# A sparse feed-forward layer whose first matmul writes features on partitions

## Chip, cores, metric

The kernel runs on one core of a Trainium2 chip. The metric is the device time of one execution in microseconds; the median of several runs counts. The kernel is written by hand: each engine (TensorE for matmuls, called PE in the profile; VectorE, DVE; ScalarE, ACT; GpSimd, POOL; SyncE, SP) has its own list of instructions, and semaphores tie them together.

## The reference

A small transformer of eight sub-layers, each adding to x (16 sequences, 112 positions, 256 features) what it makes of layernorm(x): cross-attention (0), feed-forward (1), attention (2), feed-forward (3), attention (4), feed-forward (5), attention (6), feed-forward (7). Sub-layers 1, 5 and 7 are mixtures of 8 experts, and they are what the change touches:

```
sub-layer 1: expert = argmax of the router,    F = 1024, func = gelu
sub-layer 5: the best two experts of 8,        F = 512,  func = silu
sub-layer 7: expert = argmax of the router,    F = 256,  func = gelu
out = weight * (func(x @ W1[e] + b1[e]) @ W2[e] + b2[e])      W1: 256 x F, W2: F x 256
```

The reference computes all experts for all rows; the kernel computes for each row only the experts it is sent to.

## The kernel before

`route_phase` makes the layernorm, the router's choice, and stores each row's 256 features in DRAM as two float16 parts (HI, and LO, the rest). `experts_phase` sorts the rows by expert into tiles of 128 rows that belong to one expert each: NT is 21 tiles in sub-layer 1, 35 in sub-layer 5 and 21 in sub-layer 7. Which expert a tile has is known only at run time: PE loads its number into a register (`value_load`, L2449) and every access to the expert's weights is addressed through a register (`bass.ds(e, 1)`).

For each tile j the engines do this:

- POOL gathers 128 rows from DRAM (`gather`, L2335), XR + 3 tiles ahead.
- PE turns the gathered rows (`turn_x`, L2363: four transposes of 128x128 in float16), and DVE copies them out of PSUM to `x16` (`take_x`, L2535): features on partitions, in HI and LO parts.
- `hidden` (L2372 to L2388): for each block of BW = min(F, 512) hidden features, one matmul that adds the bias (`add_bias`, L2368 or L2370, with 2 or 16 partitions), and six matmuls (x LO by w HI, x HI by w LO, x HI by w HI, each in two halves of the 256 features). The stationary operand is `x16` (128x128), the moving one the weights w1h, BW columns. The result in PSUM has rows on partitions.
- ACT applies the function (`apply`, L2469) into `hs`, which lies in the space of XT.
- The result has to be turned before the second layer, since its features must be on partitions. For F = 1024 `turn_h` (L2407) turns the float32 result in 8 transposes, ACT takes the HI part from PSUM (`high_h`, L2490), DVE the LO part (`low_h`, L2551). For F = 512 and 256 (`early`) ACT and DVE first make the two float16 parts (`high_parts` L2476, `low_parts` L2539), PE turns both (`turn_parts`, L2396, 2F/128 transposes), and ACT and DVE copy them out (`take_high` L2482, `take_low` L2545) to `h16`.
- `output` (L2411 to L2427): F/128 matmuls of 512 columns (L2420), a bias matmul (L2368 or L2370) and F/128 matmuls of 256 columns (L2424), with `h16` stationary and w2h moving.
- ACT copies half of the result (`half_y`, L2496), DVE adds the other (`add_y`, L2558), POOL scatters the rows to DRAM (L2346).

The order of each engine's work is written out by hand in its loop over j. On PE it is: load the expert of tile j, `turn_x(j + 1)`, `hidden(j)`, turn the result of tile j - 1, `output(j - 2)`. In between ACT and DVE also turn the experts' weights, which SP loads as float32, into the float16 parts: `make_high` (L2064) on ACT and `make_low` (L2070) on DVE, four pieces per expert for F = 1024 and two otherwise.

Of the kernel before, what the change touches and what calls it, by code (L numbers as in the profile page):

```python
# [16 lines left out]
DC = D // 128  # L17
# [2228 lines left out]
def experts_phase(nc, tag, X, XT, ident, r, w, xnd, ytd, func, xn=None, out=None):  # L2246
# [5 lines left out]
    HR, YR = 3, 3  # L2252
# [3 lines left out]
    with ExitStack() as st:  # L2256
# [17 lines left out]
        h16 = m.sb("h16", [128, 2, 2, F], F16)  # L2274
        y2 = m.sb("y2", [128, 2, D])
        if F == 1024:
            xs = XT[:, 1, 1024:1024 + XR * D].bitcast(F16).rearrange("p (r d) -> p r d", d=2 * D)
            y = XT[:, 0, 1024:1024 + YR * D].rearrange("p (r d) -> p r d", d=D)
        else:
            xs, y = m.sb("xs", [128, XR, 2 * D], F16), m.sb("y", [128, YR, D])  # L2280
            hk = m.sb("hk", [128, 2, 2, F], F16)
# [10 lines left out]
        t_bank = [(m.bank16 if early else m.bank)(f"t{i}") for i in range(2)]  # L2292
# [8 lines left out]
        turned, x_ready, h_done, h_made, t_done, h_hi, h_low, o_done, y_half, y_done, x_done, added = (  # L2301
            m.sem(n) for n in ("turned", "x_ready", "h_done", "h_made", "t_done", "h_hi", "h_low", "o_done", "y_half",
                               "y_done", "x_done", "added"))
        hk_hi, hk_low, ready16, stored = m.sem("hk_hi"), m.sem("hk_low"), m.sem("ready16"), m.sem("stored")
# [5 lines left out]
        with nc.Block() as block:  # L2310
# [42 lines left out]
            def _(pe):  # L2353
# [17 lines left out]

                def hidden(j):  # L2372
                    e = experts[j]
                    pe.wait_ge(x_ready, j + 1)
                    pe.wait_ge(w.split, upto(min(j, E - 1) - 1) + w.first)
                    for blk in range(NB):
                        n = j * NB + blk
                        bank = h_bank[n % HR]
                        cols = slice(blk * BW, (blk + 1) * BW)
                        if n >= HR:  # L2380
                            pe.wait_ge(h_made, n - HR + 1)
                        add_bias(bank[:, 0:BW], e, cols, start=True, stop=False)
                        for i, (x, z) in enumerate(PARTS):
                            for c in range(DC):
                                mm = pe.matmul(bank[:, 0:BW], x16[:, j % 2, x, c, :],  # L2385
                                               w.w1h[:, z, c, bass.ds(e, 1), cols].rearrange("p o f -> p (o f)"),
                                               start=False, stop=(i, c) == (2, DC - 1))
                        mm.then_inc(h_done, 1)  # L2388

                def turn_parts(j):  # L2390
                    pe.wait_ge(hk_low, j + 1)
                    for z in (HI, LO):
                        if j >= 1:
                            pe.wait_ge((h_hi, h_low)[z], j)
                        for f in range(FC):
                            mm = pe.transpose(t_bank[z][:, f * 128:(f + 1) * 128], hk[:, j % 2, z, f * 128:(f + 1) * 128],  # L2396
                                              ident16[:, :])
                        mm.then_inc(t_done, 1)

                def turn_h(j):  # L2400
                    pe.wait_ge(h_made, (j + 1) * NB)
                    for blk in range(NB):
                        if j * NB + blk >= 2:
                            pe.wait_ge(h_low, j * NB + blk - 1)
                        for f in range(BW // 128):
                            at = blk * BW + f * 128
                            mm = pe.transpose(t_bank[(j * NB + blk) % 2][:, f * 128:(f + 1) * 128], hs[:, j % 2, at:at + 128],  # L2407
                                              ident[:, :])
                        mm.then_inc(t_done, 1)

                def output(j):  # L2411
                    e = experts[j]
                    bank = o_bank[j % 2]
                    pe.wait_ge(w.split, upto(min(j, E - 1)))
                    pe.wait_ge(h_hi, (j + 1) * NB)
                    pe.wait_ge(h_low, (j + 1) * NB)
                    if j >= 2:
                        pe.wait_ge(y_done, j - 1)
                    for f in range(FC):
                        pe.matmul(bank[:, :], h16[:, j % 2, HI, f * 128:(f + 1) * 128],  # L2420
                                  w.w2h[:, bass.ds(e, 1), f, :, :].rearrange("p o z d -> p (o z d)"), start=f == 0, stop=False)
                    add_bias(bank[:, 0:D], e, slice(F, F + D), start=False, stop=False)
                    for f in range(FC):
                        mm = pe.matmul(bank[:, 0:D], h16[:, j % 2, LO, f * 128:(f + 1) * 128],  # L2424
                                       w.w2h[:, bass.ds(e, 1), f, HI, :].rearrange("p o d -> p (o d)"), start=False,
                                       stop=f == FC - 1)
                    mm.then_inc(o_done, 1)  # L2427
# [19 lines left out]
                for j in range(NT + 2):  # L2447
                    if j < NT:
                        experts[j] = pe.value_load(tile_expert[0:1, j:j + 1], min_val=0, max_val=E - 1)  # L2449
                    if j + 1 < NT:  # L2450
                        turn_x(j + 1)
                    if j < NT:
                        hidden(j)
                    if 1 <= j < NT + 1:
                        (turn_parts if early else turn_h)(j - 1)
                    if j >= 2:
                        output(j - 2)

            @block.scalar
            def _(act):  # L2460
                def apply(j):
                    if j >= 2 and early:
                        act.wait_ge(hk_low, j - 1)
                    elif j >= 2:
                        act.wait_ge(t_done, (j - 1) * NB)
# [6 lines left out]
                def high_parts(j):  # L2472
                    act.wait_ge(h_made, j + 1)
                    if j >= 2:
                        act.wait_ge(t_done, 2 * (j - 1))
                    act.copy(hk[:, j % 2, HI, :], hs[:, j % 2, :]).then_inc(hk_hi, 1)  # L2476

                def take_high(j):
                    act.wait_ge(t_done, 2 * j + 1)
                    if j >= 2:  # L2480
                        act.wait_ge(o_done, j - 1)
                    act.copy(h16[:, j % 2, HI, :], t_bank[HI][:, 0:F]).then_inc(h_hi, 1)  # L2482

                def high_h(j):
                    if j >= 2:
                        act.wait_ge(o_done, j - 1)
                    for blk in range(NB):
                        n = j * NB + blk
                        act.wait_ge(t_done, n + 1)
                        act.copy(h16[:, j % 2, HI, blk * BW:(blk + 1) * BW], t_bank[n % 2][:, 0:BW]).then_inc(h_hi, 1)  # L2490
# [11 lines left out]
                for j in range(NT + 2):  # L2502
# [3 lines left out]
                    if j < NT:  # L2506
                        apply(j)
                        if early:
                            high_parts(j)
                    if 1 <= j < NT + 1:  # L2510
                        (take_high if early else high_h)(j - 1)
                    if j >= 2:
                        half_y(j - 2)
# [5 lines left out]
            def _(dve):  # L2519
# [17 lines left out]
                def low_parts(j):  # L2537
                    dve.wait_ge(hk_hi, j + 1)
                    dve.tensor_tensor(hk[:, j % 2, LO, :], hs[:, j % 2, :], hk[:, j % 2, HI, :], ALU.subtract).then_inc(hk_low, 1)  # L2539

                def take_low(j):
                    dve.wait_ge(t_done, 2 * j + 2)
                    if j >= 2:
                        dve.wait_ge(o_done, j - 1)
                    dve.tensor_copy(h16[:, j % 2, LO, :], t_bank[LO][:, 0:F]).then_inc(h_low, 1)  # L2545

                def low_h(j):
                    for blk in range(NB):
                        n = j * NB + blk
                        dve.wait_ge(h_hi, n + 1)  # L2550
                        dve.tensor_tensor(h16[:, j % 2, LO, blk * BW:(blk + 1) * BW], t_bank[n % 2][:, 0:BW],  # L2551
                                          h16[:, j % 2, HI, blk * BW:(blk + 1) * BW], ALU.subtract).then_inc(h_low, 1)
# [91 lines left out]
                for j in range(NT + 2):  # L2644
# [5 lines left out]
                    if early and j < NT:  # L2650
                        low_parts(j)
                    if 1 <= j < NT + 1:
                        (take_low if early else low_h)(j - 1)
                    if j >= 2:
                        add_y(j - 2)
# [139 lines left out]
```

## Time and profile before

| | |
|---|---|
| median of 3 runs | 2612.92 us (2605.26 to 2613.96) |
| the profiled execution's own time | 2597.31 us |
| its span | 2595.4 us |
| granted TensorE clock over the span | 0.917 of full speed |
| PE, DVE, ACT, POOL busy | 85%, 61%, 53%, 37% |
| experts' tiles of sub-layer 1 on PE | 331 to 490 us |
| of sub-layer 5 | 1999 to 2145 us |
| of sub-layer 7 | 2518 to 2575 us |

In the profile PE is the matmul side of TensorE and PEld its weight loads, which overlap with matmuls. A matmul's duration holds its way through the array, so durations of neighbours overlap; what counts is the distance from one start to the next.
### The profile page before, as it was taken

How to read it: one execution, taken by the hardware profiler on the slowest of the kernel's cores; microseconds unless marked ns; L12 is line 12 of the kernel's file. 1: busy time of each engine (PE TensorE's matmuls, PEld its weight loads, DVE VectorE, ACT ScalarE, POOL GpSimd, SP SyncE). 2: the span in 40 equal slices, each digit the busy share in tenths (PEclk: the TensorE clock that was granted, in tenths of full speed). 3: DMA queues.
4: the chain of work that ended last, by engine and by line, in shares of the span. 5: the costliest groups of instructions: out<-in, count | busy, mean ns of one | idle time of the engine just before them, and what ended most of it. 6: DMA issues, size and time to landing. Idle time of an engine off the chain costs nothing. (4 is left out here: it accounts for less than half of the span.)

```text
span 2595.4 us, 62474 instructions
## 1 busy us (share of the span) xinstructions
PE 2197.0 (85%) x23896; PEld 1460.3 (56%) x23896; DVE 1573.8 (61%) x3664; ACT 1381.3 (53%) x2919; POOL 955.7 (37%) x1066
## 2 busy tenths in 40 slices
PE   4888499689999999958689999999974993899846
PEld 2556245367777777745546666666652551466524
DVE  3667572476665656636767777777765644555465
ACT  2666463265555555524366666666653652566634
POOL 3543132154454444403423333333313742433135
PEclk7999699899999999968889999999986996899958
DMA  5663271310000000010200000000023224432034
GB/s 118 118 111 78 87 237 35 106 36 14 14 8 14 14 14 2 2 33 1 81 14 15 14 15 9 15 14 9 2 71 95 78 60 113 98 79 68 21 110 127
DMA packets 118580, 139.57 MB, mean 54 GB/s; under 512 B 15072, under 2 KB 107184, under 8 KB 118288
## 3 DMA queue, kind: packets, MB, share of 16 engines
q1 hardware_dynamic: 110900, 115.39, 17.3%
q0 software_dynamic: 7392, 20.19, 2.5%
q8 instruction: 199, 3.26, 0.6%
q14 instruction: 89, 0.73, 0.1%
HBM read 93.25 MB, written 17.47 MB: 43 GB/s over the span
## 5 line engine op out<-in xcount | busy, mean ns | idle before, releaser
L915 DVE TENSOR_REDUCE a_mx<-a_pair 112x2 f32<-112x750 f32 x256 | 237.9, 936 | 196.0 <-PE a_pair L984 196.0
L1223 POOL TENSOR_TENSOR a_kp<-a_kp 125x512 f16<-125x512 f32 x192 | 217.6, 1159 | 259.1 <-ACT a_kp L1314 259.1
L316 POOL TENSOR_SCALAR a_P<-a_P,a_inv 112x375 f32<-112x375 f32 x256 | 148.9, 595 | 378.1 <-DVE a_inv L447 377.0
L853 ACT ACTIVATE a_PT<-a_pair 125x672 f32<-125x672 f32 x256 | 186.3, 731 | 69.9 <-PE a_pair L996 65.2
L354 ACT ACTIVATE a_P<-a_masked,a_least 112x375 f32<-112x375 f32 x256 | 153.4, 600 | 83.5 <-DVE a_least L442 81.6
L1357 DVE SCALAR_TENSOR_TENSOR a_k<-a_p,a_k 128x375 f16<-128x375 f32 x128 | 69.3, 547 | 138.9 <-ACT a_k L1270 138.8
L1314 ACT CAST a_kp<-a_kp 125x512 f16<-125x512 f32 x192 | 110.4, 617 | 76.4 <-DVE a_kp L1376 76.4
L535 PE MATMUL a_p<-a_kc,a_wk 128*128 128x375 f16 x768 | 147.0, 327 | 4.1 <-POOL a_kc L310 4.1
L1456 PE MATMUL a_p<-a_kc,a_wk 128*128 128x375 f16 x768 | 142.2, 327 | 5.4 <-POOL a_kc L1215 5.4
L442 DVE CUSTOM_DVE_ANT_0 a_masked<-a_s,a_mask_add 112x375 f32<-112x375 f32 x256 | 129.9, 545 | 27.1 <-PE a_s L572 26.1
L549 PE MATMUL a_p<-a_wv,a_kc 128*125 128x512 f16 x576 | 141.9, 383 | 5.2 <-DVE a_v L481 3.6
L1456 PE MATMUL a_p<-a_wv,a_kc 128*125 128x512 f16 x576 | 141.0, 385 | 0.0
L2385 PE MATMUL f_hb<-w_w1h,f_x 128*128 x588 | 136.7, 371 | 0.0
L2469 ACT ACTIVATE all_XT<-f_hb 128x512 f32<-128x512 f32 (+1 forms) x98 | 53.3, 550 | 152.6 <-PE f_hb L2385 151.4
L1376 DVE TENSOR_SCALAR a_kp<-a_p 125x512 f32<-125x512 f32 x192 | 122.8, 681 | 8.2 <-PE a_p L1487 8.2
L472 DVE SCALAR_TENSOR_TENSOR a_k<-a_p,a_k 128x375 f16<-128x375 f32 x128 | 70.3, 549 | 82.7 <-ACT a_k L365 82.7
L582 PE MATMUL a_t<-all_ident,a_P 112*125 112x112 f32 x768 | 116.5, 288 | 3.4 <-POOL a_P L316 3.4
L452 DVE TENSOR_TENSOR a_PT<-a_t,a_PT 125x336 f16<-125x336 f32 x256 | 116.8, 498 | 1.4 <-ACT a_PT L390 1.4
L582 PEld LDWEIGHTS a_t<-all_ident,a_P 112*125 112x125 f32 x768 | 93.8, 188 | 38.8 <-issue 34.6
L1015 PE MATMUL a_y<-a_PT,a_values 125*32 125x112 f32 x3072 | 102.4, 267 | 5.4 <-ACT a_PT L853 5.3
L549 PEld LDWEIGHTS a_p<-a_wv,a_kc 128*125 128x125 f16 x576 | 77.8, 137 | 49.7 <-DVE a_k L472 6.8
L996 PE MATMUL a_pair<-a_q,a_k 50*125 50x112 f16 (+1 forms) x1536 | 89.2, 223 | 19.5 <-DMA a_q<-a_mT 10.9
(420 smaller groups left out, 5271.1 us busy)
## 6 DMA issues: line engine op xcount, KB each, us to landing
a_kc<-in_ctxT SPq DMA_DIRECT2D x64, 375.0 KB, 3.4
a_k<-a_k_parts SPq DMA_DIRECT2D x192, 93.8 KB
w_stage<-in_L_ffn_W SPq DMA_DIRECT2D x32, 512.0 KB, 5.5
w_stage<-in_L_ffn_ew SPq DMA_DIRECT2D x16, 512.0 KB, 5.9
w_stage<-expert_rows SPq DMA_DIRECT2D x16, 448.0 KB, 7.6
a_v_in_sb<-in_ctx SPq DMA_DIRECT2D x16, 375.0 KB
a_q<-a_q_parts SPq DMA_DIRECT2D x48, 112.0 KB, 3.5
w_stage<-in_L_ffn_W SPq DMA_DIRECT2D x16, 256.0 KB, 4.5
```

The lines of the kernel that those rows point to most:

```text
L316: pool.tensor_scalar(P[:, p % 4, r, :], P[:, p % 4, r, :], inv[:, p % 4, r:r + 1], 1.0, ALU.mult, ALU.mult).then_inc(P_done, 1)
L354: act.activation(P[:, p % 4, r, :], masked[:, p % 2, r, :], ACT.Exp, bias=least[:, p % 4, r:r + 1], scale=-1.0, accum_out=total[:, p % 4, ...
L442: dve.tensor_tensor_reduce(masked[:, p % 2, r, :], s_bank[0:S, r, 0:SK], mask_add[:, b % 2, :], 1.0, 3e38, ALU.add, ALU.min, least[:, p % ...
L535: mm = pe.matmul(out[:, 0:SK], wk16[:, z, j, c * 128:(c + 1) * 128], kc16[:, b % 2, x, j, :], start=i == j == 0, stop=(i, j) == (2, DC - 1))
L549: mm = pe.matmul(out[0:KP, 0:512], kc16[:, b % 2, x, j, jk * KP:(jk + 1) * KP], wv16[:, z, j, w * 512:(w + 1) * 512], start=i == j == 0, s ...
L582: mm = pe.transpose(t_bank[0:KP, r, j * S:(j + 1) * S], P[:, p % 4, r, j * KP:(j + 1) * KP], ident[0:S, 0:S])
L853: act.activation(PT[:, p % 4, :, :], pair_bank[slot["turned", p]][0:KP, :, 0:KT * S], ACT.Exp).then_inc(exp_done, 1)
L915: dve.tensor_reduce(mx[:, b % 2, 2 * pair:2 * pair + 2], pair_bank[slot["score", p]][0:S, :, 0:SK], AX.X, ALU.max).then_inc(max_done, 1)
L1223: pool.tensor_tensor(kp16[:, LO, j, hf, r, :, :].rearrange("p c m -> p (c m)"), kp[:, n % 4, :], kp16[:, HI, j, hf, r, :, :].rearrange("p ...
L1376: dve.tensor_scalar(kp[:, n % 4, :], p_bank[bank][0:KP, 0:512], 0.0, EPS * WS, ALU.max, ALU.add).then_inc(f_evac, 1)
L1456: mm = pe.matmul(out, lhs(x, z, j), rhs(x, z, j), start=i == j == 0, stop=(i, j) == (2, DC - 1))
L2385: mm = pe.matmul(bank[:, 0:BW], x16[:, j % 2, x, c, :], w.w1h[:, z, c, bass.ds(e, 1), cols].rearrange("p o f -> p (o f)"), start=False, st ...
```

## The change

The first layer is computed the other way round. In `hidden` the weights w1h are now the stationary operand, 128 hidden features at a time, and the 128 rows of `x16` move; so a block of 512 hidden features, seven matmuls of 512 columns before, becomes four groups of seven matmuls of 128 columns. Each group begins with its own bias matmul (`turn_bias`), whose stationary operand is the bias row and whose moving operand is a row of ones (or `r.pick`). Each group writes 128 columns of the same PSUM bank. The result has features on partitions, so `turn_h` and `turn_parts` are gone, with `hk`, the banks `t_bank`, and the copies `high_parts`, `low_parts`, `take_high` and `take_low`; `high_h` and `low_h` now make the parts from `hs` for all F. For F = 1024 the outputs run one tile behind the first layer rather than two (LATE); for F = 512 and 256 still two, with three buffers in `h16`. HR, the number of banks for the first layer, is 4 rather than 3.

```diff
@@ experts_phase
     early = F < 1024
-    HR, YR = 3, 3
+    HR, YR = 4, 3
+    LATE = 2 if early else 1
+    HB = LATE + 1
...
-        h16 = m.sb("h16", [128, 2, 2, F], F16)
+        h16 = m.sb("h16", [128, HB, 2, F], F16)
...
-            hk = m.sb("hk", [128, 2, 2, F], F16)
...
-        t_bank = [(m.bank16 if early else m.bank)(f"t{i}") for i in range(2)]
...
+                def turn_bias(out, e, cols):
+                    if w.flat:
+                        pe.matmul(out, w.rows[:, bass.ds(e, 1), cols].rearrange("z o f -> z (o f)"), ones16[:, :], start=True, stop=False)
+                    else:
+                        pe.matmul(out, w.rows[:, cols], r.pick[:, bass.ds(e, 1), :].rearrange("p o t -> p (o t)"), start=True,
+                                  stop=False)
+
                 def hidden(j):
...
-                        cols = slice(blk * BW, (blk + 1) * BW)
                         if n >= HR:
                             pe.wait_ge(h_made, n - HR + 1)
-                        add_bias(bank[:, 0:BW], e, cols, start=True, stop=False)
-                        for i, (x, z) in enumerate(PARTS):
-                            for c in range(DC):
-                                mm = pe.matmul(bank[:, 0:BW], x16[:, j % 2, x, c, :],
-                                               w.w1h[:, z, c, bass.ds(e, 1), cols].rearrange("p o f -> p (o f)"),
-                                               start=False, stop=(i, c) == (2, DC - 1))
-                        mm.then_inc(h_done, 1)
-
-                def turn_parts(j):
...
-                def turn_h(j):
...
                         for f in range(BW // 128):
                             at = blk * BW + f * 128
...
+                            out = bank[:, f * 128:(f + 1) * 128]
+                            turn_bias(out, e, slice(at, at + 128))
+                            for c in range(DC):
+                                for x, z in ((HI, HI), (LO, HI), (HI, LO)):
+                                    mm = pe.matmul(out, w.w1h[:, z, c, bass.ds(e, 1), at:at + 128].rearrange("p o f -> p (o f)"),
+                                                   x16[:, j % 2, x, c, :], start=False, stop=(c, z) == (DC - 1, LO))
+                        mm.then_inc(h_done, 1)
...
-                for j in range(NT + 2):
+                for j in range(NT + LATE):
...
                         hidden(j)
-                    if 1 <= j < NT + 1:
-                        (turn_parts if early else turn_h)(j - 1)
-                    if j >= 2:
-                        output(j - 2)
+                    if j >= LATE:
+                        output(j - LATE)
...
                 def apply(j):
-                    if j >= 2 and early:
-                        act.wait_ge(hk_low, j - 1)
-                    elif j >= 2:
-                        act.wait_ge(t_done, (j - 1) * NB)
+                    if j >= 2:
+                        act.wait_ge(h_low, (j - 1) * NB)
...
-                def high_parts(j):
...
-                def take_high(j):
...
                 def high_h(j):
-                    if j >= 2:
-                        act.wait_ge(o_done, j - 1)
+                    if j >= HB:
+                        act.wait_ge(o_done, j - HB + 1)
                     for blk in range(NB):
...
+                        act.wait_ge(h_made, j * NB + blk + 1)
+                        act.copy(h16[:, j % HB, HI, blk * BW:(blk + 1) * BW],
+                                 hs[:, j % 2, blk * BW:(blk + 1) * BW]).then_inc(h_hi, 1)
...
-                def low_parts(j):
...
-                def take_low(j):
...
                 def low_h(j):
                     for blk in range(NB):
...
+                        cols = slice(blk * BW, (blk + 1) * BW)
+                        dve.wait_ge(h_hi, j * NB + blk + 1)
+                        dve.tensor_tensor(h16[:, j % HB, LO, cols], hs[:, j % 2, cols], h16[:, j % HB, HI, cols],
+                                          ALU.subtract).then_inc(h_low, 1)
```

## Rows read from the trace of the kernel before

**Rows 1.** Windows, one each in sub-layers 1, 5, 7: PE, PEld, DVE, ACT, POOL busy, granted clock

```profile
355.00:475.00 120.00, 120.00 (x694) 63.97 (x693) 49.84 (x80) 54.22 (x97) 33.27 (x31) 1.00 0.26 84
2062.00:2130.00 68.00, 68.00 (x477) 36.42 (x476) 30.27 (x68) 35.17 (x68) 34.47 (x36) 1.00 0.22 65
2550.23:2562.15 11.92, 11.92 (x102) 7.62 (x100) 6.97 (x21) 7.17 (x21) 9.18 (x10) 1.00 0.39 106
```

**Rows 2.** Timeline of PE in one tile of sub-layer 1 (start, us, what)

```profile
460.68 0.39 PE L2363 MATMUL f_xt<-f_ident,all_XT 128*128 128x128 f16 x4
461.00 0.39 PE L2370 MATMUL f_hb<-w_rows,r_pick 16*128 16x512 f16 x1
461.32 1.47 PE L2385 MATMUL f_hb<-w_w1h,f_x 128*128 x6
...
464.34 1.04 PE L2407 MATMUL f_t<-all_ident,all_XT 128*128 128x128 f32 x8
465.21 1.89 PE L2420 MATMUL f_o<-w_w2h,f_h 128*128 x8
...
468.13 0.39 PE L2363 MATMUL f_xt<-f_ident,all_XT 128*128 128x128 f16 x4
```

**Rows 3.** Timeline of PE in one tile of sub-layer 5

```profile
2057.36 0.39 PE L2363 MATMUL f_xt<-f_ident,f_xs 128*128 128x128 f16 x4
2057.68 0.39 PE L2368 MATMUL f_hb<-w_rows,f_ones 2*128 x1
...
2059.31 0.61 PE L2396 MATMUL f_t<-f_ident,f_hk 128*128 128x128 f16 x8
2059.75 1.03 PE L2420 MATMUL f_o<-w_w2h,f_h 128*128 x4
...
2061.37 0.33 PE L2363 MATMUL f_xt<-f_ident,f_xs 128*128 128x128 f16 x3
```

**Rows 4.** Timeline of PE in one tile of sub-layer 7

```profile
2550.55 0.28 PE L2368 MATMUL f_hb<-w_rows,f_ones 2*128 x1
...
2551.43 0.39 PE L2396 MATMUL f_t<-f_ident,f_hk 128*128 128x128 f16 x4
2551.65 0.59 PE L2420 MATMUL f_o<-w_w2h,f_h 128*128 x2
...
2552.62 0.39 PE L2363 MATMUL f_xt<-f_ident,f_xs 128*128 128x128 f16 x4
```

**Rows 5.** Instructions of single lines: duration min/median/max, first and last start

```profile
L2420 PEldq FUSED_REGOPS  x8: 46/46/46, 462.9 to 463.9; - x8
...
L2385 PEld LDWEIGHTS f_hb<-w_w1h,f_x x588: 95/98/147, 331.6 to 2570.1; 128*128 128x128 f16 x196
...
L2385 PEldq FUSED_REGOPS  x392: 46/46/46, 330.8 to 2569.6; - x196
...
L2449 PEldq TENSOR_LOAD <-f_tile_expert x17: 300/302/310, 2063.1 to 2127.2; - x17
...
L2359 PEldq EVENT_SEMAPHORE  x17: 51/51/51, 2063.8 to 2127.9; - x17
```

**Rows 6.** Bias matmuls L2368 in sub-layers 5 and 7: first and last start

```profile
L2368 PE MATMUL f_hb<-w_rows,f_ones x35: 384/385/602, 1999.5 to 2137.6; 2*128 x35
...
L2368 PE MATMUL f_hb<-w_rows,f_ones x21: 277/278/391, 2518.3 to 2569.4; 2*128 x21
```

**Rows 7.** Timeline of PE in sub-layer 2: a run of short matmuls

```profile
704.04 1.25 PE L1517 MATMUL a_kvs_sum<-a_v,a_kp 125*128 125x65 f16 x36
705.22 0.75 PE L1497 MATMUL a_p<-a_q,a_pp 64*128 64x224 f16 x12
```

**Rows 8.** Groups by line of ACT and DVE, 355 to 475 us

```profile
L2064 ACT ACTIVATE w_w2h<-w_stage 128x1024 f16<-128x1024 f32 x7 | 7.4, 1061 | 5.1 <-DMA w_stage<-in_L_ffn_W 5.1
...
L2070 DVE SCALAR_TENSOR_TENSOR w_w2h<-w_stage,w_w2h 128x1024 f16<-128x1024 f32 x8 | 9.6, 1220 | 2.6 <-ACT w_w2h L2064 2.6
```

**Rows 9.** Timeline of POOL in sub-layer 7

```profile
2544.84 0.99 POOL L2346 DMA_INDIRECT expert_rows<-f_y,f_dest  x1 [0.31 <-issue]
```

More of the change, by code:

```diff
@@ L2300, in experts_phase @@
         got_in = [m.sem(f"got_in{i}") for i in range(G)]
-        turned, x_ready, h_done, h_made, t_done, h_hi, h_low, o_done, y_half, y_done, x_done, added = (
-            m.sem(n) for n in ("turned", "x_ready", "h_done", "h_made", "t_done", "h_hi", "h_low", "o_done", "y_half",
+        turned, x_ready, h_done, h_made, h_hi, h_low, o_done, y_half, y_done, x_done, added = (
+            m.sem(n) for n in ("turned", "x_ready", "h_done", "h_made", "h_hi", "h_low", "o_done", "y_half",
                                "y_done", "x_done", "added"))
-        hk_hi, hk_low, ready16, stored = m.sem("hk_hi"), m.sem("hk_low"), m.sem("ready16"), m.sem("stored")
+        ready16, stored = m.sem("ready16"), m.sem("stored")
         def upto(e):
@@ L2388, in hidden @@
-                        mm.then_inc(h_done, 1)
-                def turn_parts(j):
[L2391 to L2398, printed above, removed]
@@ L2400, in turn_h @@
-                def turn_h(j):
[L2401 to L2404, printed above, removed]
                         for f in range(BW // 128):
                             at = blk * BW + f * 128
-                            mm = pe.transpose(t_bank[(j * NB + blk) % 2][:, f * 128:(f + 1) * 128], hs[:, j % 2, at:at + 128],
-                                              ident[:, :])
-                        mm.then_inc(t_done, 1)
+                            out = bank[:, f * 128:(f + 1) * 128]
@@ L2419, in output @@
                     for f in range(FC):
-                        pe.matmul(bank[:, :], h16[:, j % 2, HI, f * 128:(f + 1) * 128],
+                        pe.matmul(bank[:, :], h16[:, j % HB, HI, f * 128:(f + 1) * 128],
                                   w.w2h[:, bass.ds(e, 1), f, :, :].rearrange("p o z d -> p (o z d)"), start=f == 0, stop=False)
@@ L2423, in output @@
                     for f in range(FC):
-                        mm = pe.matmul(bank[:, 0:D], h16[:, j % 2, LO, f * 128:(f + 1) * 128],
+                        mm = pe.matmul(bank[:, 0:D], h16[:, j % HB, LO, f * 128:(f + 1) * 128],
                                        w.w2h[:, bass.ds(e, 1), f, HI, :].rearrange("p o d -> p (o d)"), start=False,
@@ L2470, in apply @@
                                        scale=1.0 / WS).then_inc(h_made, 1)
-                def high_parts(j):
-                    act.wait_ge(h_made, j + 1)
-                    if j >= 2:
-                        act.wait_ge(t_done, 2 * (j - 1))
-                    act.copy(hk[:, j % 2, HI, :], hs[:, j % 2, :]).then_inc(hk_hi, 1)
-                def take_high(j):
-                    act.wait_ge(t_done, 2 * j + 1)
-                    if j >= 2:
-                        act.wait_ge(o_done, j - 1)
-                    act.copy(h16[:, j % 2, HI, :], t_bank[HI][:, 0:F]).then_inc(h_hi, 1)
                 def high_h(j):
-                    if j >= 2:
-                        act.wait_ge(o_done, j - 1)
+                    if j >= HB:
+                        act.wait_ge(o_done, j - HB + 1)
                     for blk in range(NB):
-                        n = j * NB + blk
-                        act.wait_ge(t_done, n + 1)
-                        act.copy(h16[:, j % 2, HI, blk * BW:(blk + 1) * BW], t_bank[n % 2][:, 0:BW]).then_inc(h_hi, 1)
+                        act.wait_ge(h_made, j * NB + blk + 1)
+                        act.copy(h16[:, j % HB, HI, blk * BW:(blk + 1) * BW],
+                                 hs[:, j % 2, blk * BW:(blk + 1) * BW]).then_inc(h_hi, 1)
                 def half_y(j):
@@ L2501, in _ @@
                 act.activation(warm[:, :], ident[:, 0:1], func)
-                for j in range(NT + 2):
+                for j in range(NT + LATE):
                     if not early:
@@ L2507, in _ @@
                         apply(j)
[L2508 to L2513, printed above, removed]
+                        high_h(j)
+                    if j >= LATE:
+                        half_y(j - LATE)
                     if early:
@@ L2535, in take_x @@
                     dve.tensor_copy(x16[:, j % 2, :, :, :].rearrange("p z c t -> p (z c t)"), xt_bank[:, 0:2 * D]).then_inc(x_ready, 1)
-                def low_parts(j):
-                    dve.wait_ge(hk_hi, j + 1)
-                    dve.tensor_tensor(hk[:, j % 2, LO, :], hs[:, j % 2, :], hk[:, j % 2, HI, :], ALU.subtract).then_inc(hk_low, 1)
-                def take_low(j):
[L2542 to L2545, printed above, removed]
                 def low_h(j):
                     for blk in range(NB):
[L2549 to L2552, printed above, removed]
+                        cols = slice(blk * BW, (blk + 1) * BW)
+                        dve.wait_ge(h_hi, j * NB + blk + 1)
+                        dve.tensor_tensor(h16[:, j % HB, LO, cols], hs[:, j % 2, cols], h16[:, j % HB, HI, cols],
+                                          ALU.subtract).then_inc(h_low, 1)
                 def add_y(j):
@@ L2643, in _ @@
                 take_x(0)
-                for j in range(NT + 2):
+                for j in range(NT + LATE):
                     if j + 1 < NT:
@@ L2649, in _ @@
                             w.make_low(dve, n)
[L2650 to L2655, printed above, removed]
+                    if j < NT:
+                        low_h(j)
+                    if j >= LATE:
+                        add_y(j - LATE)
                     if early:
```

## The prediction

> **What bounds the kernel now.** I read the table of the page first, then windows over the three expert stages, then the timeline of PE in one steady tile of each, and last the single lines of PE's sequencer. The windows [rows 1] show PE busy without a gap in all three stages at a granted clock of 1.00 (the 2.4 GHz level), while DVE, ACT and POOL are busy for 28 to 77% of them. So a tile costs what PE takes for it: 468.13 - 460.68 = 7.45 us in sub-layer 1 [rows 2], 2061.37 - 2057.36 = 4.01 us in sub-layer 5 [rows 3], and 2.39 us in sub-layer 7: 2552.62 - 2550.55 = 2.07 from the bias matmul to the next `turn_x` [rows 4], and 0.32 for `turn_x`, as in the other two (461.00 - 460.68, 2057.68 - 2057.36). Only there is POOL slower: one scatter of 0.99 us with 0.31 us ahead of it, and a gather of the same size, make 2.6 us per tile [rows 9], but it catches up once the gathers are through, so PE sets the end there too.
>
> Two prices come out of these rows. Eight transposes of 128 columns take 2059.75 - 2059.31 = 0.44 us [rows 3], so a 128-column matmul costs 0.056 us start to start. In sub-layer 1 the first block's bias matmul is 0.32 us ahead of the next one, and `hidden` with its 14 matmuls lasts 464.34 - 461.00 = 3.34 us [rows 2]. With p for a 512-column matmul and s for a change of shape between the 16-partition bias and the 128-partition matmuls, p + s = 0.32 and 14p + 3s = 3.34, which gives p = 0.216 and s = 0.10. The four transposes of `turn_x`, 4 x 0.056 = 0.22, again last 0.32 up to the bias matmul: s is paid on entering and on leaving a bias matmul, with 2 partitions in sub-layer 5 and 7 as well [rows 3, 4].
>
> **The array's part of the change.** The columns that stream stay the same: 7 x 512 before, 28 x 128 after. What changes is the number of bias matmuls. A new group costs 0.056 + s, five times 0.056, and 0.056 + s to the next bias: 0.59 us. `hidden` then takes 8 x 0.59 - 0.10 = 4.61 us in sub-layer 1, 4 x 0.59 - 0.10 = 2.26 in 5, and 2 x 0.59 - 0.10 = 1.08 in 7.
> - Sub-layer 1: +1.27 against 3.34; the transposes go, 465.21 - 464.34 = 0.87 [rows 2]. Net +0.40, tile 7.85 us.
> - Sub-layer 5: +0.63 against 2059.31 - 2057.68 = 1.63; 0.44 goes [rows 3]. Net +0.19, tile 4.20 us.
> - Sub-layer 7: +0.20 against 0.88; 2551.65 - 2551.43 = 0.22 goes [rows 4]. Net 0, tile 2.37 us.
>
> So the transposes saved are paid back by six further changes of shape per 512 hidden features.
>
> **The sequencer's part.** An address that depends on the expert is computed by a FUSED_REGOPS. `hidden` has 392 of them in 98 blocks, four per block, one for each pair of z and c, and the repeated w HI addresses share theirs; `output` has eight per tile of sub-layer 1, one for each f [rows 5]. So each new constant offset costs one, and the change makes the offset depend on f as well: 4 per group, 16 per 512 features instead of 4, plus the bias's one per group where `w.rows` is addressed by expert (sub-layers 5 and 7; in 1 `r.pick` has one address per tile). Eight in a row start within 463.9 - 462.9 us, 7 distances [rows 5]: 0.13 us each with the pair of load and matmul behind it. Loading the expert's number costs 2063.8 - 2063.1 = 0.7 us up to the next wait [rows 5], and I give the four separate waits that remain (one of `turn_parts` goes) 0.13 each. Sequencer per tile:
> - Sub-layer 1: before 8 + 8 + 1 addresses, after 32 + 8 + 1: 41 x 0.13 + 0.7 + 0.5 = 6.5 us, under the array's 7.85.
> - Sub-layer 5: before 5 + 5, after 20 + 5: 25 x 0.13 + 1.2 = 4.45 us, over the array's 4.20. I take 4.40, since the distances are rounded to 0.1 us.
> - Sub-layer 7: before 5 + 3, after 10 + 3: 13 x 0.13 + 1.2 = 2.9 us, over 2.37. I take 2.80. POOL's 2.6 is now hidden.
>
> An address for a weight load is in no row (so far only moving operands have one). Below it could be free if the load needs none, above it is as dear as a moving one's; I take the upper end, the nearest row, and keep the lower one for a rival.
>
> **Waits and other engines.** ACT and DVE lose one PSUM copy each per tile in 5 and 7; in 1 the same copies read `hs`. None is late before: per tile of sub-layer 1 ACT has four pieces of 1.06 us and DVE four of 1.22 [rows 8], 4.2 and 4.9 us, with some 2.8 and 2.1 us besides, under 7.85. With outputs one tile behind, PE's `output(j - 1)` comes after `hidden(j)`, 4.6 us after `hidden(j - 1)` and `output(j - 2)`, so ACT and DVE have time to make the parts. On DVE `low_h(j)` now stands ahead of `add_y`, and behind it the next `take_x`, which PE needs only an iteration later; I cost it at nothing, covered by `output`'s 2.92 us in sub-layer 1 and 1.6 in 5 [rows 2, 3]. Without that cover it would be the length of `low_h`, an estimated 0.6 us per 512 columns, half of the 1.22 us [rows 8]. POOL and SP issue the same DMAs. The fourth first-layer bank only loosens a wait.
>
> **The sum.** Sub-layer 1: 21 x 0.40 = +8.4. In 5 the 35 tiles began on average (2137.6 - 1999.5) / 34 = 4.06 us apart [rows 6], so 34 x 0.34 = +11.6. In 7 it was (2569.4 - 2518.3) / 20 = 2.56 [rows 6], so 20 x 0.24 = +4.8. The first matmuls of a stage run at the lower clock (602 ns at most against 385 [rows 6]), with more of them in each group: +1. In all +26 us. The profiled execution took 2597.3 us, 15.6 under the median; on the median this makes 2639 us. A measurement of this kernel can tell about 0.3%, 8 us, from no change.
>
> The page "TensorE: Matmul & The Clock Gate" of the Trainium skill, section "Back-to-back issue gap", speaks against short matmuls: it gives some 81 ns for each of a stream of loads and 128-column matmuls. The trace has 56 ns in runs of eight [rows 3]. By 81 ns a group would cost 0.77 us and the sum would come to about +73 us; this belongs beside the first rival.
>
> **Rivals.**
> 1. *Weight loads set the pace* (9%). Each 128-column matmul needs its own load of 98 ns [rows 5]; if loads with an address in a register did not overlap with each other, a group would take 7 x 0.098 + 0.10 = 0.79 us. Tiles: 0.32 + 8 x 0.79 - 0.1 + 2.92 = 9.46, 0.31 + 3.06 + 1.62 = 4.99, 0.32 + 1.48 + 0.97 = 2.77 us: 21 x 2.0 + 34 x 0.93 + 20 x 0.21 = +78 us, 2691. Against it stand 36 matmuls of 65 columns with their loads in 1.18 us, 33 ns each [rows 7].
> 2. *The clock falls* (5%). The array streams for 7 x 0.053 of 0.59 us, less densely than now. At 1.2 GHz the 128-column matmul costs 0.107 and a group 0.95, 0.36 us more: tiles of 10.7, 5.6 and 3.1 us, 21 x 3.3 + 34 x 1.6 + 20 x 0.5 = +134 us, 2747. Against it: 33 ns matmuls ran at full pace in sub-layer 2 [rows 7].
> 3. *Faster* (13%): the change of shape is hidden when short matmuls stand around the bias, and the new addresses cost the sequencer nothing to speak of. A group is then 7 x 0.056 = 0.39 us. Sub-layer 1: 0.32 + 3.14 + 2.92 = 6.38, -1.07 x 21 = -22; sub-layer 5: 0.31 + 1.57 + 1.62 = 3.50, -0.56 x 34 = -19; sub-layer 7 is held by POOL, -1: -42 us, 2571. It decides once a group costs less than (3.34 + 0.87 + 0.10) / 8 = 0.54 us in sub-layer 1 and fewer than (4.06 - 1.2) / 0.13 = 22 addresses are left per tile in 5. For it speaks only that the rows have no group of this form.
> 4. *About even* (8%): changes of shape free, addresses as forecast. Sub-layer 1 is at the sequencer's 6.5, -20; 5 and 7 as forecast, +16: -4 us, 2609.
>
> If only the addresses were free, it would be +8.4 + 0.14 x 34 + 0 = +13 us; that lies in the forecast's own range, +12 to +45 us (upper end: sequencer and array hinder each other by 0.3 us per tile).
>
> **How the numbers follow.** The forecast has 65%. The range starts at 2608, between the even case and the forecast, which leaves out the faster rival, and reaches to 2685, short of the loads' full price: some 19% outside. Faster by over 0.3%: 0.13. Slower: forecast, loads and clock, 79%, less 4% of the forecast that ends within 8 us: 0.75. Same: 0.12.
>
> **What would show it.** On PE's timeline a tile of sub-layer 1 should take 7.85 us, of 5 4.4 and of 7 2.8; groups of L2370/L2368 and six matmuls should come every 0.59 us in sub-layer 1 and 0.65 in 5. FUSED_REGOPS of `hidden` should number 16 x 77 + 8 x 21 = 1400, with PE idle "issue" in 5 and 7. The page of lines should have no f_t. Groups of 0.39 us would make me wrong towards faster, loads 98 ns apart or a clock under 0.9 in these stages towards slower.

## The result, and the profile after

The changed kernel takes 2636.11 us in the median of four runs (2633.73 to 2642.45) against 2609.09 us before: 1.0111 times as estimated from all runs, 95% interval [1.0094, 1.0129] (the two medians alone divide to 1.0104). The change makes the kernel 1% slower. The prediction was 2639 against 2613, 1.0100 times. The profiled execution of the change took 2635.8 us with a span of 2633.7.

One tile of sub-layer 1 on PE's timeline, where [rows 2] stood before:

```profile
412.92 0.39 PE L2363 MATMUL f_xt<-f_ident,all_XT 128*128 128x128 f16 x4
413.24 0.22 PE L2376 MATMUL f_hb<-r_pick,w_rows 16*128 x1
413.39 0.51 PE L2394 MATMUL f_hb<-f_x,w_w1h 128*128 128x128 f16 x6
413.83 0.23 PE L2376 MATMUL f_hb<-r_pick,w_rows 16*128 x1
...
417.93 1.89 PE L2407 MATMUL f_o<-w_w2h,f_h 128*128 x8
...
420.84 0.39 PE L2363 MATMUL f_xt<-f_ident,all_XT 128*128 128x128 f16 x4
```

A group of seven comes every 413.83 - 413.24 = 0.59 us, 0.15 to 0.16 us of it from the bias matmul to the next and as much back again, where 0.056 us would do without a change of shape. `hidden` takes 417.93 - 413.24 = 4.69 us (forecast 4.61), `output` still 2.91, the tile 7.92 us (forecast 7.85, before 7.45). The transposes are gone (0.87 us), but `hidden` is 1.35 us longer: the six further changes of shape per 512 hidden features cost more than the transposes did.

The weight loads show where a change of shape costs its time. These are loads of the change, then of the padded kernel e3 below, in which no matmul changes the shape:

```profile
413.23 0.09 PEld L2376 LDWEIGHTS f_hb<-r_pick,w_rows 16*128 16x128 f16 x1
413.39 0.34 PEld L2394 LDWEIGHTS f_hb<-f_x,w_w1h 128*128 x6
```

```profile
405.67 0.10 PEld L2382 LDWEIGHTS f_hb<-r_pick,w_rows 128*128 128x128 f16 x1
405.73 0.38 PEld L2400 LDWEIGHTS f_hb<-f_x,w_w1h 128*128 x6
```

In e3 each load starts some 0.055 us ahead of its own matmul (405.73 and 405.78 on PE), right behind the start of the matmul before it. In the change the loads at 413.23 and 413.39 start at the same time as their matmuls: at a change of shape the load is not made ahead, and that holds for the bias matmul's load and for the one after it.

One tile of sub-layer 5, for [rows 3], and the lines of the first layer, for [rows 5]:

```profile
2077.53 0.39 PE L2363 MATMUL f_xt<-f_ident,f_xs 128*128 128x128 f16 x4
2077.85 0.23 PE L2374 MATMUL f_hb<-f_ones,w_rows 2*128 2x128 f16 x1
...
2080.24 1.03 PE L2407 MATMUL f_o<-w_w2h,f_h 128*128 x4
...
2081.86 0.39 PE L2363 MATMUL f_xt<-f_ident,f_xs 128*128 128x128 f16 x4
```

```profile
L2394 PEld LDWEIGHTS f_hb<-f_x,w_w1h x2100: 95/98/151, 330.0 to 2608.8; 128*128 x191
...
L2394 PEldq FUSED_REGOPS  x1400: 46/46/46, 329.5 to 2608.7; - x175
```

Addresses number 1400, as forecast, and this tile takes 4.33 us, others of the second half of the stage up to 4.62; the median of 34 distances is 4.45 (forecast 4.40, before 4.01). The loads keep their 98 ns with an address in a register. In the steady tiles of sub-layers 1 and 5 neighbours within a group are 0.056 us apart in the median, so neither short matmuls nor such loads are slow in themselves.

What was not forecast stands at the start of sub-layer 1. Windows of the kernel before, then of the changed one (start and end, length, PE, PEld, DVE, ACT, POOL busy, granted clock, DMA):

```profile
331.00:337.00 6.00, 6.00 (x17) 1.75 (x16) 5.59 (x8) 0.60 (x1) 0.95 (x1) 0.54 0.53 158
337.00:343.00 6.00, 6.00 (x37) 3.07 (x36) 4.36 (x5) 4.98 (x6) 0.96 (x1) 1.00 0.91 297
343.00:350.00 7.00, 7.00 (x42) 3.77 (x41) 6.74 (x8) 6.33 (x11) 0.00 (x0) 1.00 0.95 312
```

```profile
331.00:337.00 6.00, 6.00 (x45) 4.12 (x46) 3.81 (x4) 0.60 (x1) 0.04 (x1) 0.50 0.73 231
337.00:343.00 6.00, 6.00 (x47) 4.12 (x45) 4.18 (x8) 5.42 (x8) 0.96 (x1) 0.50 0.48 165
343.00:350.00 7.00, 7.00 (x44) 4.07 (x44) 4.00 (x5) 2.40 (x7) 0.00 (x0) 0.67 0.89 293
```

Both begin at the lower level, 1.2 GHz. Before, the clock is at 2.4 GHz (1.00) from 337 us on; with the change it stays at 0.50 until after 343, though PE counts as busy in both. At the lower level a group takes 0.97 us rather than 0.60.

### The profile page after: what moved, and what is told of

It is laid out like the page before. It is cut to its first block and busy times, and to the rows that moved or that the text cites. A ratio compares the mean times of both kernels' runs of the same rounds, so it can differ in the third digit from the quotient of the medians.

```text
span 2633.7 us, 65801 instructions
## 1 busy us (share of the span) xinstructions
PE 2230.4 (85%) x25128; PEld 1515.7 (58%) x25128; DVE 1558.2 (59%) x3608; ACT 1357.7 (52%) x2863; POOL 953.6 (36%) x1066
## 5 line engine op out<-in xcount | busy, mean ns | idle before, releaser
L2394 PE MATMUL f_hb<-f_x,w_w1h 128*128 128x128 f16 x2100 | 191.8, 231 | 0.6 <-issue 0.5
L2509 DVE TENSOR_TENSOR f_h<-all_XT,f_h 128x512 f16<-128x512 f32 (+1 forms) x98 | 60.3, 634 | 195.9 <-ACT f_h L2460 175.7
L2394 PEld LDWEIGHTS f_hb<-f_x,w_w1h 128*128 x2100 | 127.9, 102 | 27.6 <-issue 1.0
```

Of the source, the lines that this page charges most:

```text
L2394: mm = pe.matmul(out, w.w1h[:, z, c, bass.ds(e, 1), at:at + 128].rearrange("p o f -> p (o f)"), x16[:, j % 2, x, c, :], start=False, stop= ...
```

## The experiments

Seven kernels ran, in two groups, each on one chip; the kernel before took 2594.07 us beside the first four and 2607.06 beside the last three, so runs of different groups are compared by their ratios. This table has from each profile the median tile (distance from one `turn_x` to the next) and the length of each stage, from the start of the first `turn_x` to the end of the last `output`, in us, and the ratio of the times to the kernel before with its interval:

| | sub-layer 1 | sub-layer 5 | sub-layer 7 | ratio |
|---|---|---|---|---|
| before | 7.45, 163.6 | 4.01, 155.5 | 2.38, 59.9 | |
| change, first profile | 7.93, 178.8 | 4.45, 172.3 | 3.18, 74.8 | 1.0111 [1.0094, 1.0129] |
| e1 change again | 7.93, 179.1 | 4.45, 172.2 | 2.83, 68.9 | 1.0141 [1.0121, 1.0161] |
| e2 fixed expert | 7.93, 177.7 | 4.23, 165.5 | 2.39, 60.9 | 1.0095 [1.0075, 1.0114] |
| e3 change, padded | 6.71, 149.0 | 4.45, 168.1 | 2.79, 63.7 | 1.0017 [1.0003, 1.0030] |
| e4 before, padded | 6.83, 151.5 | 3.59, 143.0 | 2.33, 57.8 | 0.9902 [0.9874, 0.9931] |
| e5 e3 and one bias address | 6.71, 149.1 | 4.07, 158.4 | 3.24, 74.3 | 0.9946 [0.9929, 0.9962] |
| e6 e4, new form in 1 | 6.72, 149.2 | 3.59, 142.6 | 3.00, 69.7 | 0.9876 [0.9853, 0.9899] |
| e7 all one behind | 7.93, 178.4 | 4.47, 170.8 | 3.22, 74.4 | 1.0127 [1.0104, 1.0150] |

**e1, the change again.** No edit.

> The changed kernel once more, as a control. Theory (shape changes of 0.10 us around each bias matmul bound sub-layer 1, address computation bounds 5 and 7): tiles of 7.93, 4.43 and about 2.8 us; 2636 us. The first profile's sub-layer 7 had tiles of 2.7 to 4.7 us; if that comes from something that varies from run to run, these tiles differ here while those of 1 and 5 stay; if it belongs to the kernel, the same long tiles are at the same places.

2630.99 us. Sub-layers 1 and 5 repeat to 0.3 us. In 7 the long tiles of the first profile are not there: its second half runs at 2.73 to 2.87 us per tile. So the forecast 2.8 us is the kernel's, and the rest varies from run to run.

**e2, addresses constant.** It leaves out the choice of expert in the first layer, in 5 and 7 for the bias too.

```diff
-                        pe.matmul(out, w.rows[:, bass.ds(e, 1), cols].rearrange("z o f -> z (o f)"), ones16[:, :], start=True, stop=False)
+                        pe.matmul(out, w.rows[:, 0, cols], ones16[:, :], start=True, stop=False)
...
-                                    mm = pe.matmul(out, w.w1h[:, z, c, bass.ds(e, 1), at:at + 128].rearrange("p o f -> p (o f)"),
+                                    mm = pe.matmul(out, w.w1h[:, z, c, min(j, E - 1), at:at + 128],
...
```

> The first layer's weights (and in sub-layers 5 and 7 its bias) are those of expert min(j, 7) rather than of the tile's expert, so the first layer is that of another expert for most tiles and its addresses are constants. Theory: sub-layer 1 is bound by the array and stays at 7.9 us per tile; sub-layer 5 falls from 4.43 to the array's 4.2 us, sub-layer 7 from 2.8 to POOL's 2.6 us or a little under; about 2618 us. Rival (loads with an address in a register are slow in themselves): sub-layer 1 falls as well, by over 0.3 us per tile.

2618.82 us, 12 less than e1. Sub-layer 1 stays at 7.93, 5 falls to the array's 4.23 and 7 to 2.39. That is under POOL's 2.6, as it is in the kernel before (2.38): PE goes ahead of POOL while gathered tiles are in store. The addresses cost 0.22 us per tile in 5 and 0.4 in 7, nothing in 1.

**e3, no change of shape.** All operands of bias matmuls have 128 partitions, those beyond the bias filled with zeros.

```diff
-        self.pick = m.sb("pick", [2 * E, E, 128], F16)
+        self.pick = m.sb("pick", [128, E, 128], F16)
...
-        self.rows = m.sb("rows", [2, E, F + D] if self.flat else [2 * E, F + D], F16)
+        self.rows = m.sb("rows", [128, E, F + D] if self.flat else [128, F + D], F16)
...
+        pool.memset(self.rows[:], 0.0).then_inc(self.rows_blank, 1)
...
-        ident16, ones16, warm = m.sb("ident16", [128, 128], F16), m.sb("ones16", [2, 128], F16), m.sb("warm", [128, 1])
+        ident16, ones16, warm = m.sb("ident16", [128, 128], F16), m.sb("ones16", [128, 128], F16), m.sb("warm", [128, 1])
...
```

> The change with the operands of all bias matmuls filled up with zeros to 128 partitions, so that no matmul changes the shape of the array. Theory: groups of 0.39 us (7 x 0.056), the array would need 6.1 us in sub-layer 1, so that the sequencer's 6.5 us is the bound there; sub-layers 5 and 7, bound by the sequencer already, stay at 4.4 and 2.8. Together 21 x 1.4 = 30 us less than the change, 2606 us. Rival (short matmuls or their loads cost the time, not the shape): groups stay over 0.55 us and the time within 5 us of the change.

2597.94 us, 33 less than e1 (forecast 30). PE's timeline in sub-layer 1:

```profile
405.73 0.22 PE L2382 MATMUL f_hb<-r_pick,w_rows 128*128 x1
405.78 0.50 PE L2400 MATMUL f_hb<-f_x,w_w1h 128*128 128x128 f16 x6
406.12 0.22 PE L2382 MATMUL f_hb<-r_pick,w_rows 128*128 x1
```

The group is 0.39 us, as forecast to the hundredth. The tile is 6.71 rather than 6.5: the last groups of a tile come 0.5 us and more apart, as PE waits for addresses. Sub-layer 5 keeps 4.45, bound by the sequencer alone now. This row has eight addresses of one stretch of sub-layer 1:

```profile
L2400 PEldq FUSED_REGOPS  x8: 46/46/46, 400.6 to 401.5; - x8
```

By the trace's single starts (400.641 to 401.510) they are 0.124 us apart, although each lasts 46 ns, and the step is the same whether one pair of load and matmul stands between two of them or two. Some steps of a tile are longer, 0.15 to 0.28 us. In sub-layer 5 the 25 addresses make 3.1 of the 4.45 us; loading the expert's number takes 0.65 of the rest.

And the windows at the start of sub-layer 1, which here begins at 319.5 us:

```profile
319.00:326.00 7.00, 2.72 (x25) 2.49 (x26) 2.31 (x5) 1.06 (x1) 4.11 (x4) 0.50 0.61 208
326.00:332.00 6.00, 5.54 (x80) 4.97 (x78) 5.45 (x10) 3.81 (x6) 0.95 (x1) 0.94 0.82 262
```

The clock is up 7 us after the first `turn_x`, where the change took 23 and the kernel before 11. The matmuls are those of the change, in the same order; only the padding differs, and with it the pauses.

**e4, the same padding in the kernel before.** The edit of e3, nothing else.

> The kernel before with the same zeros in the bias operands and nothing else. Theory: six changes of shape of 0.10 us go per tile of sub-layer 1 (7.45 to 6.85 us), four in 5 (4.01 to 3.6), four in 7 (2.39 to 2.0, where POOL's 2.6 takes over): 13 + 14 + 1 us less than before, 2581 us. Rival (the 0.10 us comes from the bias matmul's other operands or its address, not from its few partitions): no change, 2609 us.

2566.80 us, 27 less than before (forecast 28). Tiles are 6.83, 3.59 and 2.33 us, the stages 12.1, 12.5 and 2.1 us shorter. In 7 PE gains 0.05 us per tile where the four changes of shape would give 0.4. It is not POOL's 2.6 that holds it, as the expectation had it, but the sequencer: in steady tiles its instructions follow one another without a pause, eight addresses of 0.124 us and some 1.3 us for the expert's number and the waits, 2.3 us in all.

**e5, one bias address per tile.** On e3: `self.flat = False` for all sub-layers.

> The padded change, with the bias rows of sub-layers 5 and 7 laid out as in sub-layer 1 (a fixed row block, chosen by r.pick): one address per tile for all bias matmuls instead of five or three. Theory (each address costs the sequencer 0.125 us, and it is the bound in 5 and 7): tiles of sub-layer 5 fall from 4.45 to 3.95 us, of 7 from 2.8 to POOL's 2.6 us, sub-layer 1 stays at 6.74; some 20 us less than the padded change, ratio to before about 0.993. Rival (something else on the array bounds 5): no change against the padded change, ratio 1.002.

2592.63 us. The ratio falls from e3's 1.0017 to 0.9946, some 18 us (forecast 20). Sub-layer 5 falls from 4.45 to 4.07 us, 0.095 per address taken away rather than 0.125. The other addresses keep their step of 0.124 us in the trace; what stands against the gain is a register instruction more per tile (ALU_OP, 0.05 us) and some steps of 0.17 to 0.22 us. The two profiles can't show where all 18 us come from: the stage of sub-layer 5 is 10 us shorter than in e3, but sub-layer 7, disturbed in this profile, 11 us longer, and e3's profiled execution (2587.95 us) was 10 us under that kernel's median.

**e6, the new form in sub-layer 1 alone.** On e4: the weights stationary, no `turn_h`, outputs one tile behind for F = 1024.

> The padded old kernel with the new first layer (weights stationary, no turning, outputs one tile behind) in sub-layer 1 alone. Theory: with shape changes gone the new form is bound by the sequencer there, 6.74 us per tile against the old form's 6.83, so 21 x 0.09 = 2 us less than the padded old kernel, ratio to before about 0.989; sub-layers 5 and 7 keep 3.59 and 2.35 us. Rival (with the shape changes gone, doing without transposes gains their 0.87 us): 18 us less, ratio 0.983.

2574.72 us, ratio 0.9876; the interval overlaps e4's, so the two can't be told apart by their times. The stage of sub-layer 1 is 2.3 us shorter than in e4, as forecast, not 18: the new form is held by its 41 addresses there. Both padded kernels, e4 and e6, are 1% under the kernel before.

**e7, distance of the outputs.** `LATE = 1` for all.

> The change with outputs one tile behind in sub-layers 5 and 7 as well. Theory: ACT and DVE make the parts of tile j in about 2 us in sub-layer 5 and 1.3 us in 7 while PE works for 2.7 and 1.4 us on the next tile's first layer, so tiles stay at 4.45 us, and sub-layer 7 stays at 2.8 or gains up to 0.3 us of waiting; 0 to +6 us against the change. Rival (the distance of the outputs is what costs or saves time): tiles of 5 change by over 0.2 us.

2636.41 us, ratio 1.0127. Tiles of 5 are 4.47 us against 4.45: how far behind the outputs run neither costs nor saves time there. Sub-layer 7 was disturbed in this profile and says nothing of it.

## Why the prediction was right

- *Price of a change of shape, 0.10 us each way.* Right: groups of 0.59 us in the change, 0.39 in e3, and 0.6 us per tile of sub-layer 1 gained in e4 for six changes, 0.4 in 5 for four. That the bias matmul's few partitions are the reason, and not its other operands, is shown by e3 and e4, which change nothing else in these matmuls.
- *Transposes saved.* Right in size: the tile of sub-layer 1 grew by 0.48 us, `hidden` by 1.35, and the 0.87 between them are the transposes. e3 and e6 show why the saving is not kept even without changes of shape: the sequencer becomes the bound at 6.7 us.
- *Sequencer as the bound of 5 and 7.* Right: 4.45 against 4.40 and 2.8 against 2.80, and e2 brings back the array's 4.23 and 2.39. The price in it was partly luck: 1.0 us over 7 distances [rows 5] reads 0.14 us, not 0.13, which would have made 4.7 us. The address costs 0.124, and the rest of a tile 1.35 us rather than 1.2.
- *An address for a weight load is as dear as for a moving operand.* Right at its upper end: both kinds stand 0.124 us apart in e3, and without those of the first layer the tiles of 5 and 7 are the array's again (e2).
- *LATE.* Nothing in sub-layer 5, as costed (e7). The copies saved on ACT and DVE, and the fourth bank, were not tested by themselves; in steady tiles PE was busy throughout in sub-layer 1 (120 of 120 us), so they could have given nothing there.
- *The first matmuls at the lower clock, +1 us.* This term was too small. e1's stages are longer by 179.1 - 163.6 = 15.5, 16.7 and 9.0 us, 41 us in all, where the sum had 8.4, 11.6 and 4.8. In sub-layer 1 the steady tiles explain 21 x 0.48 = 10 us; the other 5 come from its first two tiles, whose 16 groups all run at the lower clock, 0.97 us each rather than 0.60, with the first output behind them (3 + 3 + 2 us), where before it was one tile (2.5 us). I had taken the length of the stretch at the lower clock as given, while it changed with the kernel.
- *The base of sub-layers 5 and 7.* The sum set a steady tile after (4.40, 2.80) against an average before that contains the slow first tiles (4.06, 2.56). But the first tiles are slow after the change too. Steady against steady it is 4.45 - 4.01 = 0.44 us and 2.80 - 2.38 = 0.42 us per tile, not 0.34 and 0.24, which makes some 15 and 8 us; the rest of the 16.7 and 9.0 stands in the first tiles.
- *The total.* That it came out to a microsecond is luck: 26 us was forecast, the runs give 27 in the first measurement, 37 in the second (e1) and 29 for the near twin e7, and the stages of e1's profile 41. Of those 41 the span shows 2629.8 - 2595.4 = 34, mostly because sub-layer 6, which the change does not touch, took 363.0 us in e1's profile and 369.0 in that of before. It goes with the clock there and not with the kernel: in five profiles (the change, e1, e4, e5, e7) the mean granted clock over sub-layer 6 was 0.87 to 0.88 and its length 363.0 to 366.0 us, in the other four 0.85 to 0.86 and 368.2 to 369.2.
- *Rivals.* Slow loads and slow short matmuls: refuted by the 0.056 us within groups and by e3. The falling clock: wrong for steady tiles (1.00 over 355 to 475 us), right in kind at the start of each stage; its price left out that `output` and `turn_x` double too (e1's first `output` took 4.69 us rather than 2.91). Both faster ones: the shape changes were not hidden. The bottom of the range, 2608, lies just below the even case of 2609 and not, as the prediction has it, between that and the forecast.

Open is what stretches single tiles in the later part of sub-layer 7 in four profiles (the first, e5, e6, e7) and not in the other five. The same kernel shows it and does not, and e6 shows it in a stage whose code is e4's. In exactly these four, ACT there waits for a semaphore that the profile puts on no engine of the program, 2.9 to 4.2 us at the longest, and the granted clock falls back to 0.50 within the stage. In the first profile the waits come first, with tiles of 3.64 and 4.66 us; the clock is at 0.50 from 2576.6 to 2586.8 us, and the two tiles of 4.02 and 4.07 us in it are what tiles at the lower clock take (e1's, before its clock rose, took 4.02 to 4.07). What ACT waits for I did not find.

## What to carry to other kernels

Count changes of operand shape, not only columns: here a matmul of 2 or 16 partitions between matmuls of 128 cost 0.20 us beyond its own time, and zeros up to 128 partitions took that away. Where operands are addressed by a run-time index, count the distinct offsets: each cost the sequencer 0.124 us here, so cutting one 512-column matmul with a run-time address into four of 128 columns can move the bound from the array to the instruction stream. Before turning a layer round to save transposes, check both; here the padding alone, in the old form, brought 1% (e4), and the turned form cost 1.0 to 1.4%.

## What the runs showed of the hardware that was not expected

The stretch at the lower clock at the start of sub-layer 1 was longer in every profile with changes of shape. After the first `turn_x` the clock was up in 7 to 10 us in the four padded kernels (7.2, 7.3, 9.7, 7.8 in e3, e4, e5, e6), in 10.5 us with a bias matmul of 16 partitions in every seven of 512 columns (before), and in 22 to 25 us with one in every seven of 128 columns (the change 23.4, e1 24.6, e2 21.7, e7 23.2). In these last four it rose only after the first layer's groups had ended, 0.8 to 3.7 us into the first `output`. In sub-layer 5 the order is much the same, 12 to 14 us against 15.5 and 19 to 26 (in e3 and e5 it fell back again behind that); in 7 the ranges meet. The padding removes the pauses of 0.1 us and also lets the bias matmuls use 128 partitions; which of the two moves the clock is not separated. In e1 it was still down here:

```profile
343.00:350.00 7.00, 7.00 (x41) 4.06 (x40) 5.76 (x6) 3.87 (x6) 0.00 (x0) 0.50 0.65 199
350.00:360.00 10.00, 10.00 (x92) 6.24 (x90) 6.68 (x8) 6.27 (x9) 2.03 (x2) 0.95 0.62 214
```
